# Writing a window mask on the score products' own 64x32 tiles instead of on 64x128 tiles

## The chip, the cores and the metric

One core of a Trainium2 chip (trn2). The metric is the device time of one execution in microseconds (us). TensorE has its own row in the profile for matmuls (PE) and one for weight loads (PEld), which overlap.

## The reference

The input is x of 8 sequences, 256 tokens, 128 channels. First comes one pre-norm causal attention with 16 heads of 8 channels and position slopes. Then the main part, six layers deep, each with local attention and a feed-forward:

```python
# attn_layer, per layer, 16 heads of 64
q, k, v = split(shift_tokens(x) @ Wqkv, 3)
q, k = l2norm(q) * q_scale, l2norm(k) * k_scale        # then rotary tables
# local_attention, windows of 32 queries, each sees its own 32 keys and the 32 before
mask = (it < jb) | (it > jb + w) | (jb == -1)
sim = einsum('bhwie,bhwje->bhwij', bq, bk2) * 8.0
sim = where(mask, -finfo.max, sim)
out = einsum('bhwij,bhwje->bhwie', softmax(sim), bv2)
x = out @ Wo + x
# ffn_layer: layernorm, W1, gelu gate, W2, + x
```

What matters here is `sim` with its mask: a query of a window may see at most 64 keys, of which the mask takes about half away, and in the first window of a sequence also the missing keys before it.

## The kernel before, in words

All loops are written out by Python, so the program is one long straight line of instructions for each engine; there is no loop on the chip. The setup part (lines 212 to 1178) computes the first attention and folds weights. The main part handles 48 units, one for each layer and sequence (`UNITS = L * B`), in a software pipeline: `pipeline` calls `step` for s from -1 to 50, and each engine's `step` names, by hand and in a fixed order, which piece of which unit comes next. Four units are under way at a time: `after` (s + 1), `u` (s), `before` (s - 1) and `last` (s - 2).

A unit has 256 tokens in two tiles of 128 tokens, called the first tile (t = 0) and the second tile (t = 1) here. For each tile TensorE does:

- `proj` (lines 1767 to 1790): a 128x512 piece of the q, k or value projection, as three products (lines 1784, 1785, 1786) that accumulate in one PSUM bank;
- `transpose_qk` (line 1801): four 128x128 transposes of the rotated q or k, which ScalarE copies to `qT` and `kT` (`copy_qkT`, lines 1590 and 1594);
- `scores` (lines 1804 to 1823): the masked scores of the tile in two PSUM banks, `SO[t]` and `SO[t] + 1`, one for the even and one for the odd heads (`hp`);
- `transpose_p` (line 1831) and `values` (line 1842): transposes of the probabilities and their products with the values, on 128x32 tiles;
- the feed-forward of an older unit (lines 1853 to 1903).

In `scores` a pair of heads lies on the 128 partitions, head `hp` on partitions 64 hp to 64 hp + 63. A window of 32 queries fills 32 columns of the array, so a score product takes 64 rows and 32 columns of it: eight such 64x32 tiles exist, two row halves by four column tiles `k`, and 8 pairs of heads `a` times 4 windows `k` times 2 halves `hp` make 64 products of 64 columns each. They don't start from zero. Before them, the mask is written to the whole of both banks by two products, one for each row half, with a one-hot matrix `wpick` (bf16) that picks for each of the 128 queries its row of the mask table `wmask` (bf16, 8 x 64 = 512 columns). These open the accumulation (`start=True`), and the scores add to it (`start=False`).

The waits at the head of `scores` (lines 1809 and 1811) are for the last copy to `kT` of this tile by ScalarE (`qkT_a`) and for the copy of the attention output out of the same banks for the unit before (`o_a`). At its end one signal (`sc_p`) releases `soft_top` on VectorE (line 1422), the row maximum of the scores; then follow subtraction (line 1431), exponential on ScalarE (line 1602), sum (line 1439) and scaling on VectorE. In TensorE's hand-written order `scores(u, 0)` stands at line 1948 between `proj(u, 1, 6)` and `proj(u, 1, 7)`, and `scores(u, 1)` at line 1969 between `proj(after, 0, 4)` and `proj(after, 1, 4)`.

Of the kernel before, what the change touches and what calls it, by code (L numbers as in the profile page):

```python
# [83 lines left out]
def build(nc, x, w_heads, bq_heads, bk_heads, w_v, b_v_rows, w_proj, b_proj_rows, wqk, q_scale_rows, k_scale_rows, wvt, wo,  # L84
          feed_cols, w1, w2, rope, ident, win_mask, win_pick, causal, positions, slope_heads, one_row, weights, out):
    with ExitStack() as ctx:
        def sb(name, shape, dt=F32):
            return ctx.enter_context(nc.sbuf_tensor(name, shape, dt))
# [4 lines left out]
        ps = ctx.enter_context(nc.psum_tensor("ps", [P, 8, 512], F32))  # L93
# [10 lines left out]
        wmask = sb("wmask", [P, PAIRS, 2 * WIN], BF16)  # L104
        wpick = sb("wpick", [P, TT, P], BF16)
# [36 lines left out]
        PJ, SO, TP, FB = 0, (2, 4), 6, 7  # L142
# [1049 lines left out]
        def index(u):  # L1192

            return u[0] * 2 + u[1]
# [5 lines left out]
        def live(u):  # L1200

            n = index(u)
            return not isinstance(n, int) or 0 <= n < UNITS
# [7 lines left out]
        with nc.Block() as block:  # L1211
# [531 lines left out]
            def _(pe):  # L1743
                M = nc.tensor
# [59 lines left out]
                def scores(u, t):  # L1804

                    if not live(u):
                        return
                    n, par = index(u), u[1] % 2
                    pe.wait_ge(qkT_a.sem, qkT_a.at(n, 4 * t + 3))
                    if not (isinstance(n, int) and n < 1):  # L1810
                        pe.wait_ge(o_a.sem, o_a.at(n - 1, t))
                    for hp in range(2):
                        rows = slice(64 * hp, 64 * hp + 64)
                        M.matmul(ps[:, SO[t] + hp, :], wpick[rows, t, :], wmask[rows, :, :].rearrange("p a k -> p (a k)"), start=True, stop=False)  # L1814
                    for a in range(PAIRS):
                        for k in range(4):
                            w = 4 * t + k
                            for hp in range(2):
                                rows = slice(64 * hp, 64 * hp + 64)
                                out_s = ps[32 * k:32 * k + 32, SO[t] + hp, a * 2 * WIN:(a + 1) * 2 * WIN]  # L1820
                                last = M.matmul(out_s, qT[rows, par, a, 32 * w:32 * w + 32], kT[rows, a, 32 * w:32 * w + 64],  # L1821
                                                start=False, stop=a == PAIRS - 1)
                    last.then_inc(sc_p.sem, 1)
# [259 lines left out]
```

## Time and profile before

| | |
|---|---|
| three runs | 1713.82, 1719.82, 1723.14 us; median 1719.82 |
| span of the profiled execution, its own time on the profiler | 1711.8 us |
| TensorE matmuls (PE) | busy 1660.6 us, 97% of the span, 26531 records |
| weight loads (PEld) | busy 1330.2 us, 78% |
| VectorE (DVE) | busy 1480.6 us, 86% |
| ScalarE (ACT) | busy 1268.7 us, 74% |
| GpSimd (POOL) | busy 1283.8 us, 75% |
| mean granted clock of TensorE | 0.991 |

The profile comes from one execution; its span runs from the first to the last instruction, and the time of a run has what lies around the span on top. For the profiled execution no other time than the span is given. Durations of single matmuls overlap on the array, so on PE the distance from one start to the next tells what a product costs. A float32 product shows as two records (64 score products as 128), a bf16 product or a float32 transpose as one.

### The profile page before, as it was taken

What the parts mean: (1) busy time and instruction counts of PE and PEld (TensorE: products, weight loads), DVE (VectorE), ACT (ScalarE), POOL (GpSimd) and SP (SyncE); (2) the same over time, 40 slices, a digit from 0 to 9 for tenths busy, and PEclk for the clock granted to TensorE, in tenths of its full rate; (3) what the DMA queues carried; (4) which work ended last, traced back from release to release, by engine and by line L of the source; (5) the groups of instructions that cost most, each with busy time, mean ns of one, the idle gap of its engine ahead of it and who ended that gap; (6) DMA issues with size and microseconds to landing.
All of it is one profiled execution on the core that took longest, in us unless ns stands there. A gap on an engine that the chain in (4) does not pass through costs nothing.

```text
span 1711.8 us, 65044 instructions
## 1 busy us (share of the span) xinstructions
PE 1660.6 (97%) x26531; PEld 1330.2 (78%) x26531; DVE 1480.6 (86%) x2313; ACT 1268.7 (74%) x2639; POOL 1283.8 (75%) x1744
## 2 busy tenths in 40 slices
PE   7999959999999999999999999999999999999997
PEld 5777637878888888888788888888878887888885
DVE  6887748989999999999889999999989898999984
ACT  6888746767777777777777777777777777777774
POOL 7787568777777877777778777787877777777770
PEclk9999979999999999999999999999999999999999
DMA  3588516564866656765567756658565567656654
GB/s 123 189 289 315 183 37 150 123 149 105 241 136 147 147 116 152 207 158 135 125 141 196 168 138 137 143 121 236 123 161 127 132 142 205 155 132 138 143 119 118
DMA packets 101385, 265.43 MB, mean 155 GB/s; under 512 B 26720, under 2 KB 34912, under 8 KB 101088
## 3 DMA queue, kind: packets, MB, share of 16 engines
q1 hardware_dynamic: 101088, 261.26, 60.6%
q8 instruction: 211, 3.46, 0.9%
q14 instruction: 86, 0.70, 0.1%
HBM read 45.15 MB, written 27.26 MB: 42 GB/s over the span
## 4 chain that ended last, share of the span: by engine, by line
PE 80%; issue 2%; SPq 1%; DVE 1%; ACT 1%; POOL 1%; DMA 1%; ACTq 0%; DVEq 0%; POOLq 0%
PE ps L1784 12%; PE ps L1801 10%; PE ps L1786 10%; PE ps L1842 10%; PE ps L1785 10%; PE ps L1821 8%; PE ps L1892 7%; PE ps L1831 5%; PE ps L1903 4%; PE ps L1814 2%; SPq L1228 1%; PE ps L1861 1%; PE ps L1869 1%; PE ps L1853 1%; PE ps L1878 1%
## 5 line engine op out<-in xcount | busy, mean ns | idle before, releaser
L1312 POOL TENSOR_TENSOR rot<-rot 128x512 f32<-128x512 f32 x380 | 480.7, 1287 | 99.6 <-DVE rot L1411 99.6
L1411 DVE TENSOR_TENSOR rot<-ps,rope_l 128x1024 f32<-128x1024 f32 x380 | 463.3, 1221 | 48.2 <-ACT sq L1568 33.4
L1578 ACT ACTIVATE un<-ps 128x512 f32<-128x512 f32 x384 | 229.5, 598 | 238.1 <-PE ps L1786 205.3
L1784 PE MATMUL ps<-w_t,xs_hi 128*128 128x512 f32 x764 | 377.4, 494 | 19.2 <-PEq L362 11.0
L1355 POOL TENSOR_TENSOR rot<-rot,rnorm 128x1024 f32<-128x1024 f32 x190 | 362.1, 1906 | 21.4 <-POOL rnorm L1339 0.4
L1786 PE MATMUL ps<-w_t,xs_lo 128*128 128x512 f32 x764 | 303.4, 397 | 0.4 <-issue 0.4
L1785 PE MATMUL ps<-w_t,xs_hi 128*128 128x512 f32 x764 | 301.5, 395 | 1.6 <-issue 1.6
L1568 ACT ACTIVATE sq<-ps 128x512 f32<-128x512 f32 x380 | 227.0, 601 | 60.3 <-PE ps L1786 59.9
L1397 DVE TENSOR_REDUCE ssum<-sq 128x16 f32<-128x1024 f32 x190 | 230.8, 1215 | 27.4 <-ACT sq L1568 27.4
L1801 PE MATMUL ps<-ident_s,rot 128*128 128x128 f32 x1536 | 236.9, 277 | 3.3 <-ACT kT L1594 1.7
L1801 PEld LDWEIGHTS ps<-ident_s,rot 128*128 128x128 f32 x1536 | 178.5, 140 | 52.1 <-issue 22.6
L1784 PEld LDWEIGHTS ps<-w_t,xs_hi 128*128 128x128 f32 x764 | 144.4, 189 | 64.0 <-DVE rot L1411 18.3
L1842 PE MATMUL ps<-vk,pT 128*32 128x128 f32 x6144 | 187.6, 274 | 0.8 <-ACT pT L1611 0.8
L1842 PEld LDWEIGHTS ps<-vk,pT 128*32 128x32 f32 x6144 | 161.8, 110 | 17.2 <-issue 15.7
L1786 PEld LDWEIGHTS ps<-w_t,xs_lo 128*128 128x128 f32 x764 | 144.1, 189 | 34.9 <-issue 1.2
L1785 PEld LDWEIGHTS ps<-w_t,xs_hi 128*128 128x128 f32 x764 | 145.9, 191 | 11.7 <-issue 2.4
L1821 PEld LDWEIGHTS ps<-kT,qT 64*32 64x32 f32 x12288 | 133.8, 106 | 27.1 <-issue 26.3
L1821 PE MATMUL ps<-kT,qT 64*32 64x64 f32 x12288 | 151.1, 227 | 3.2 <-issue 3.2
L1422 DVE TENSOR_REDUCE smax<-ps 128x16 f32<-128x1024 f32 x96 | 117.6, 1225 | 42.2 <-PE ps L1821 42.2
L1892 PE MATMUL ps<-xg,w_s 128*128 128x256 f32 (+1 forms) x576 | 149.6, 383 | 0.7 <-DVE hid L1487 0.3
L1439 DVE TENSOR_REDUCE lsum<-ps 128x16 f32<-128x1024 f32 x96 | 116.6, 1215 | 3.2 <-ACT ps L1602 3.2
L1431 DVE TENSOR_TENSOR prob<-ps,smax 128x1024 f32<-128x1024 f32 x96 | 117.1, 1220 | 1.5
(139 smaller groups left out, 3013.9 us busy)
## 6 DMA issues: line engine op xcount, KB each, us to landing
vk<-un SPq DMA_DIRECT2D x1440, 128.0 KB
w_t<-weights_dram SPq DMA_DIRECT2D x48, 512.0 KB, 6.5
weights_dram<-rot SPq DMA_DIRECT2D x12, 1024.0 KB, 5.2
weights_dram<-sq SPq DMA_DIRECT2D x24, 512.0 KB, 4.3
raw<-wqk_dram SPq DMA_DIRECT2D x24, 256.0 KB, 4.5
wvt_s<-wvt_dram SPq DMA_DIRECT2D x12, 256.0 KB, 5.3
wo_s<-wo_dram SPq DMA_DIRECT2D x12, 256.0 KB, 5.8
w_s<-w_dram SPq DMA_DIRECT2D x6, 341.0 KB
```

The costliest lines, as they stand in the source:

```text
L1312: last = G.tensor_tensor(cos[:, :, s, :], cos[:, :, s, :], sin[:, :, 1 - s, :], ALU.add)
L1355: G.tensor_tensor(v, v, rnorm[:, t, kind * H:(kind + 1) * H, None].broadcast_to([P, H, D]), ALU.mult).then_inc(nrm_g.sem, 1)
L1397: V.tensor_reduce(ssum[:, t, kind * H:(kind + 1) * H], sq[:, kind, :].rearrange("p (h e) -> p h e", h=H), AX_X, ALU.add).then_inc(ss_d.sem, 1)
L1411: V.tensor_tensor(dst, src[:, None, :, :].broadcast_to([P, 2, H // 2, D]), tab[:, :, None, :].broadcast_to([P, 2, H // 2, D]), ALU.mult).t ...
L1578: S.activation(un[:, (u[1] % 2) * TT + t, j // 2, (j % 2) * HALF:(j % 2 + 1) * HALF], ps[:, PJ + PJ_BANK[t][QK_BANKS + j], :], ACT.Copy).t ...
L1784: M.matmul(bank, x_hi, w_t[:, j, 0, :], start=True, stop=False)
L1785: M.matmul(bank, x_hi, w_t[:, j, 1, :], start=False, stop=False)
L1786: last = M.matmul(bank, x_lo, w_t[:, j, 0, :], start=False, stop=True)
L1801: last = M.transpose(ps[:, TP, a * P:(a + 1) * P], rot[:, kind, 0, c * P:(c + 1) * P], ident_s[:, :])
L1821: last = M.matmul(out_s, qT[rows, par, a, 32 * w:32 * w + 32], kT[rows, a, 32 * w:32 * w + 64], start=False, stop=a == PAIRS - 1)
L1842: last = M.matmul(ps[32 * k:32 * k + 32, SO[t], 0:C], pT[:, a, 32 * k:32 * k + 32], vk[:, 4 * t + k, a, :], start=a == 0, stop=a == PAIRS - 1)
L1892: last = M.matmul(ps[0:rows, feed_bank(n, i), g * T:(g + 1) * T], w1_s[:, g * DI + at:g * DI + at + rows], xg[:, :], start=True, stop=True)
```

## The change

The two mask products of a tile become eight. Each writes the mask for one window (`k`) and one row half (`hp`), on the 64x32 tile of the array on which the score products of that window and half follow, to 32 partitions of the same bank. The moving operand is the same, all 512 columns of it, in each. The values written are the same, the order of everything else too; all waits and signals stay.

```diff
@@ scores(u, t)
                     pe.wait_ge(qkT_a.sem, qkT_a.at(n, 4 * t + 3))
                     if not (isinstance(n, int) and n < 1):
                         pe.wait_ge(o_a.sem, o_a.at(n - 1, t))
-                    for hp in range(2):
-                        rows = slice(64 * hp, 64 * hp + 64)
-                        M.matmul(ps[:, SO[t] + hp, :], wpick[rows, t, :], wmask[rows, :, :].rearrange("p a k -> p (a k)"), start=True, stop=False)
+                    for k in range(4):
+                        for hp in range(2):
+                            rows = slice(64 * hp, 64 * hp + 64)
+                            M.matmul(ps[32 * k:32 * k + 32, SO[t] + hp, :], wpick[rows, t, 32 * k:32 * k + 32],
+                                     wmask[rows, :, :].rearrange("p a k -> p (a k)"), start=True, stop=False)
                     for a in range(PAIRS):
                         for k in range(4):
                             w = 4 * t + k
```

## Rows read from the trace of the kernel before

**Rows 1.** The page, part 1: busy us (share of the span) and instructions.

```profile
PE 1660.6 (97%) x26531; PEld 1330.2 (78%) x26531; DVE 1480.6 (86%) x2313; ACT 1268.7 (74%) x2639; POOL 1283.8 (75%) x1744
```

**Rows 2.** The page, part 4: the chain that ended last, by engine and line.

```profile
PE 80%; issue 2%; SPq 1%; DVE 1%; ACT 1%; POOL 1%; DMA 1%; ACTq 0%; DVEq 0%; POOLq 0%
```

**Rows 3.** A steady stretch: length, then busy us of PE, PEld, DVE, ACT, POOL.

```profile
500.00:600.00 100.00, 99.99 (x1650) 82.38 (x1652) 91.97 (x109) 76.92 (x138) 79.21 (x103) 1.00 0.62 143
```

**Rows 4.** PE by line and shape: total busy us, mean ns | idle before.

```profile
L1821 PE MATMUL ps<-kT,qT 64*32 64x64 f32 x12288 | 151.1, 227 | 3.2 <-issue 3.2
L1814 PE MATMUL ps<-wmask,wpick 64*128 64x512 bf16 x192 | 37.8, 391 | 0.0
```

**Rows 5.** Timeline, PE, a first-tile block: start, us to last end, engine, line, operation.

```profile
811.33 0.39 PE L1785 MATMUL ps<-w_t,xs_hi 128*128 128x512 f32 x1
811.56 0.40 PE L1786 MATMUL ps<-w_t,xs_lo 128*128 128x512 f32 x1
811.89 0.39 PE L1814 MATMUL ps<-wmask,wpick 64*128 64x512 bf16 x2
812.21 1.48 PE L1821 MATMUL ps<-kT,qT 64*32 64x64 f32 x128
813.62 0.50 PE L1784 MATMUL ps<-w_t,xs_hi 128*128 128x512 f32 x1
```

**Rows 6.** The same block, line 1821 alone, in short windows (records touching each window).

```profile
812.19:812.27 0.08, 0.06 (x8) 0.07 (x14) 1.00 0.00 0
812.27:812.33 0.06, 0.06 (x15) 0.06 (x23) 1.00 0.00 0
```

**Rows 7.** Timeline, PE: transposes (1831, 1801) and values (1842).

```profile
807.33 0.60 PE L1801 MATMUL ps<-ident_s,rot 128*128 128x128 f32 x4
807.86 1.95 PE L1842 MATMUL ps<-vk,pT 128*32 128x128 f32 x64
...
818.01 1.03 PE L1831 MATMUL ps<-ident_s,prob 128*128 128x128 f32 x8
818.89 0.38 PE L1801 MATMUL ps<-ident_s,rot 128*128 128x128 f32 x2
```

**Rows 8.** Timeline, ACT: the copy of kT ahead of four blocks.

```profile
270.83 0.60 ACT L1594 ACTIVATE kT<-ps 128x512 f32<-128x512 f32 x1
...
616.05 0.59 ACT L1594 ACTIVATE kT<-ps 128x512 f32<-128x512 f32 x1
...
810.43 0.60 ACT L1594 ACTIVATE kT<-ps 128x512 f32<-128x512 f32 x1
...
1669.76 0.59 ACT L1594 ACTIVATE kT<-ps 128x512 f32<-128x512 f32 x1
```

**Rows 9.** Timeline, PE: three blocks, each with what follows its scores.

```profile
272.38 1.48 PE L1821 MATMUL ps<-kT,qT 64*32 64x64 f32 x128
273.79 0.51 PE L1784 MATMUL ps<-w_t,xs_hi 128*128 128x512 f32 x1
...
617.34 1.63 PE L1821 MATMUL ps<-kT,qT 64*32 64x64 f32 x128
618.89 0.51 PE L1784 MATMUL ps<-w_t,xs_hi 128*128 128x512 f32 x1
...
1670.41 0.39 PE L1814 MATMUL ps<-wmask,wpick 64*128 64x512 bf16 x2
1670.73 1.70 PE L1821 MATMUL ps<-kT,qT 64*32 64x64 f32 x128
1672.36 0.33 PE L1853 MATMUL ps<-ident_s,o 128*128 128x128 f32 x1
```

**Rows 10.** Timeline, PE: a stall in a first-tile block; the page, part 3: instruction fetches.

```profile
873.92 1.36 PE L1821 MATMUL ps<-kT,qT 64*32 64x64 f32 x114
876.07 0.34 PE L1821 MATMUL ps<-kT,qT 64*32 64x64 f32 x14 [0.78 <-issue]
...
q8 instruction: 211, 3.46, 0.9%
```

## The prediction

> **What bounds the kernel now.** I read first the busy shares, then the chain of work that ended last, then the steady stretches, and last the timeline of TensorE around one scores block. TensorE is busy for 97% of the span, with DVE at 86% next [rows 1]; PE holds 80% of the chain [rows 2]; in a steady stretch of 100 us it is busy for 99.99 us at the full granted clock (1.00, which is 2.4 GHz), and DVE for 92 [rows 3]. So TensorE sets the end, and what a block costs there is its start to start distance on PE, not its durations, which overlap: the two mask products read 391 ns each, 37.8 us in all, and the score products 227 ns each, 151.1 us in all with 128 records per block, two for each of its 64 products [rows 4]. A step has two blocks: the first tile (t = 0) and the second (t = 1), 96 in the kernel, 48 of each.
>
> One block of the first tile reads as follows [rows 5]. The last projection product starts at 811.56, where its neighbours stand 0.23 us apart (811.33 to 811.56). The mask pair starts at 811.89, so 0.33 later: 0.10 more than a neighbour's distance. The scores start at 812.21, 0.32 after the pair, though both mask products started together and 512 columns take 0.23. That is 0.09 more. After the 128 score records the next projection starts at 813.62. The same excess stands where transposes on the full array are followed by values on 128x32 tiles: eight transposes take 0.88 to the next block of the same shape (818.01 to 818.89), so 0.11 each, but four take 0.53 to the first value product (807.33 to 807.86), which is 0.09 over 4 x 0.11 [rows 7]. I read it as the price of a change of tile shape, some 0.09 each (estimate). So today a block pays for three changes: full array to 64x128, 64x128 to 64x32, 64x32 to full array.
>
> **The change, part by part.** (1) The change of shape between mask and scores goes. Before: 0.32 us from first mask product to first score product. After: the stream alone, 0.23 by the projection rows [rows 5], since each score tile then waits only for the mask on its own 64x32 tile. The nearest row for what could be added is the first weight load on a small tile, which nothing covers: 8 score records lie in the first 0.08 us, and 7 of the next round are in by 0.06 later (x15 counts those still running too) [rows 6], so 0.02. If the masks pay it in the scores' place the scores' first round loses it, and nothing is added in sum; if both pay it, the gain is 0.07; if the bf16 stream is a little shorter than the projection's and the scores' load is covered as well, 0.10. I take 0.09, the middle, with ends 0.07 and 0.10. The two other changes of shape stay, at the price that they have.
>
> (2) Six more products and six more weight loads per block, 12 instructions, 1152 in all. On the array they cost nothing if the eight run side by side, four column tiles in each of two row halves. For it: score records on just these eight tiles start 8 in 0.08 us, with durations above 0.2 [rows 4, 6]; 64 value records of 128 columns on four column tiles take 1.95 us, 30 ns each, where full-array transposes of 128 columns need 0.11 each [rows 7]; and the mask pair on two row halves starts together. Not shown anywhere: eight streams of 512 bf16 columns at once. Bounds: nothing, and eight in line only by row half, 4 x 0.23 = 0.92 instead of 0.23. I take nothing, by the score rows, which are the same tiles.
>
> (3) The issue of those 12 instructions. The masks wait for the copy of kT by ScalarE; what follows in TensorE's queue is issued only after it. In the first tile that copy ends at 810.43 + 0.60 = 811.03, so 1.18 us before the scores start; in the second at 616.05 + 0.59 = 616.64, 0.70 before they start at 617.34 [rows 8, 9]. The block itself, from first score to next product, takes 1.41 in the first tile (813.62 - 812.21) in nearly all steps, but 1.55 in the second (618.89 - 617.34) [rows 5, 9]; going through its 48 blocks in the same view I find a few at 1.41 and most at some 0.12 over it. At the very end the lead is 0.38 (1670.35 to 1670.73) and the block 1.63; at the start one with a lead of 0.95 (271.43 to 272.38) reads 1.41 again. So with a short lead the issue falls behind the array: 0.22 late at a lead of 0.38, 0.12 at 0.70, nothing from 0.95 on. The rate: 4 + 256 instructions lie between 1670.35 and the next product at 1672.36 [rows 9]; without 0.1 for the change of shape at the end that is about 7 ns each (estimate), so 12 cost 0.085.
> First tile: lead 1.18 - 0.09 - 0.085 = 1.0, still above 0.95: no loss, gain 0.09 x 48 = 4.3 us.
> Second tile: lead 0.70 - 0.09 - 0.085 = 0.52. Between the two points (0.10 more for 0.32 less) that makes 0.06 more lateness, so the gain is 0.09 - 0.06 = 0.03, x 48 = 1.5 us. Ends: 0.09 if the lateness has another cause, and a loss of 0.085 if every instruction counts in full.
>
> (4) Nothing is added to any wait, semaphore or DMA of the data, and the waits in front of the masks stay where they are. Scores that end 0.09 earlier only feed DVE earlier, which has slack of 8 in 100 us [rows 3]; if DVE became late next, it would cost the part of 0.09 that it can't take, not more. The instructions are fetched by DMA, 16 KB at a time (3.46 MB in 211), and in some blocks PE stands for it, as 0.78 us before 876.07 [rows 10]. Going through the timeline I count some nine such stalls, about 8 us together, nearly all in or right behind a scores block. The change shifts where these pieces begin and adds 4 or 5 of them. I put it at nothing with 3 us to either side.
>
> **Sum.** 4.3 + 1.5 = 5.8 us, 0.34%. The profiled execution spans 1711.8; the three runs read 1713.82 to 1723.14, so the shortest lies 2.0 above the span and the median 8.0. I take the change from the median: 1719.8 - 5.8 = 1714.0 us. About 0.5% (8.6 us) is what a measurement of this kernel can tell from no change.
>
> **The rivals.**
> A, the forecast: full gain in the first tile, a third of it in the second. 1714.0; its own range with the ends above and the fetch's 3 us is 1708 to 1720. Chance 0.44.
> B: the second tile's lateness is not one of issue, or the queue has caught up before the scores start; both tiles gain 0.09 to 0.10, 96 x 0.095 = 9.1 us, 1710.7. For it: a few second-tile blocks already read 1.41 with the same lead. Against it: the blocks with short leads are the late ones. Chance 0.26.
> C: the issue decides the second tile in full: 48 x (0.09 - 0.085) = 0.2 us, 1719.6, no change. For it: with issue as the bound the mask's stream time is worth nothing there. Against it: the last block issues in less time than most. Chance 0.15.
> D, slower: the eight mask streams don't run side by side, so that the four column tiles of a row half follow each other. It decides in the distance from first mask to first score: above 0.32 us the change loses. At 0.92 it is 0.60 x 96 = 57.6 us more, 1777. Half way, with two at a time, 0.46 gives 13 us more, 1733. For it: the masks bring 512 columns for each weight load of 32, four copies of one stream from the same partitions, where a score product brings 64. Against it: the tiles' records of scores and values [rows 6, 7]. Chance 0.07.
> E: the shifted pieces of the code meet the dense blocks more often, twice the stalls of today, 8 - 5.8 = 2 us more, 1722, or 1727 with a stall for each of the 5 added pieces as well. For it: the blocks get denser by 12 instructions in 260. Against it: the stalls sit where the pieces happen to begin, and a shift moves as many out as in. Chance 0.05.
> F, slower too: the issue of one product with its weight load takes up to 0.06 us, which is what lies, change of shape included, between the end of the kT copy (1670.35) and the first mask product (1670.41) in the last block [rows 8, 9]. Then six more are 0.36: the second tile loses 0.36 - 0.09 = 0.27, 13 us over 48 blocks, and the first tile's lead falls to 1.18 - 0.09 - 0.36 = 0.73, where 0.1 of lateness eats its gain. 1733. Against it: 64 products are through in 1.41 us, 22 ns each with their weight loads [rows 5]. Chance 0.03.
> This is the case that the Trainium skill, "TensorE: Matmul & The Clock Gate" (in "Wait — 56ns, not 53.3ns?"), would make the likely one: it says that without hardware decoding the sequencer spends about 62 ns on each matmul, and that this binds once the array's work is shorter. By that figure the six would be 0.37 us a block. The trace doesn't agree, with its 22 ns for a product.
>
> **How the numbers follow.** The likeliest single case is A: 1714.0. Range 1706 to 1725: it takes in A, B, C and most of E with the runs' own spread of some 4 us about a median, and leaves out D, F and the tails, under 2 in 10. Faster by over 8.6 us: B's upper half and what the fetch adds to A, 0.27. Slower by over 8.6 us: D, F and the tail of E, 0.12. Within: 0.61.
>
> **What would show it.** In the timeline after, eight mask records start within 0.06 us, 0.33 behind the last projection product, and the first score 0.23 to 0.25 behind the first mask (0.32 now): step 1 and 2. If it is 0.4 or more, D. The block of the first tile stays 1.41 and that of the second grows from some 1.53 to 1.59: step 3; if it doesn't grow, B; if it grows by 0.17, C. Idle time put down to issue stays near today's. PE stays busy for 99 of 100 us in steady stretches. The prediction is wrong if PE waits for DVE more often, or if the changes of shape that stay become dearer than 0.10.

## The result, and the profile after

The changed kernel takes 1726.8 us (median of 11 runs, 1724.76 to 1735.04) against 1718.1 us for the kernel before in runs beside it: ratio 1.0061, 95% interval 1.0045 to 1.0077. The forecast was 1714.0 with a range of 1706 to 1725. So it is slower by 0.6%, where a gain of 0.3% was forecast, and it lies outside the range. A trace is of one execution: the two profiled ones differ by 12.2 us (1711.8 and 1724.0), the medians by 8.7.

The page of the changed kernel: its parts 1, 4 and 3, then a steady stretch (columns as in [rows 3]) and the two forms of the scores by line and shape (columns as in [rows 4]). The mask is now line 1815, the scores are line 1823, the values line 1844.

```profile
PE 1655.3 (96%) x27107; PEld 1340.0 (78%) x27107; DVE 1480.7 (86%) x2313; ACT 1267.7 (74%) x2639; POOL 1281.4 (74%) x1744
PE 82%; issue 2%; DVE 1%; ACT 1%; POOL 0%; ACTq 0%; DVEq 0%; POOLq 0%
q8 instruction: 216, 3.54, 0.9%
```

```profile
500.00:600.00 100.00, 99.96 (x1762) 83.17 (x1746) 92.46 (x111) 76.07 (x137) 79.89 (x107) 1.00 0.65 149
```

```profile
L1823 PE MATMUL ps<-kT,qT 64*32 64x64 f32 x12288 | 151.6, 225 | 14.9 <-issue 14.9
L1815 PE MATMUL ps<-wmask,wpick 64*32 64x512 bf16 x768 | 39.5, 389 | 0.0
```

Against [rows 1] PE has 576 more records and is busy for 5 us less in a span that is 12 us longer. The steady stretch is as full as in [rows 3]. The one row that differs plainly from [rows 4] is the idle time in front of score products: 14.9 us put down to "issue", where it was 3.2. The views of waits, PE alone, 240 to 1660 us, say how often (us in total, times, longest); first the kernel before, then the changed one:

```profile
PE ps L1821 <- issue: 3.2, 6, 0.8
```

```profile
PE ps L1823 <- issue: 14.9, 13, 2.3
```

Blocks without such a wait did what was meant. The timeline of PE in the changed kernel, a first-tile and a second-tile block:

```profile
880.35 0.40 PE L1786 MATMUL ps<-w_t,xs_lo 128*128 128x512 f32 x1
880.68 0.41 PE L1815 MATMUL ps<-wmask,wpick 64*32 64x512 bf16 x8
880.90 1.46 PE L1823 MATMUL ps<-kT,qT 64*32 64x64 f32 x128
882.29 0.50 PE L1784 MATMUL ps<-w_t,xs_hi 128*128 128x512 f32 x1
...
833.49 0.40 PE L1786 MATMUL ps<-w_t,xs_lo 128*128 128x512 f32 x1
833.82 0.41 PE L1815 MATMUL ps<-wmask,wpick 64*32 64x512 bf16 x8
834.04 1.76 PE L1823 MATMUL ps<-kT,qT 64*32 64x64 f32 x128
835.74 0.50 PE L1784 MATMUL ps<-w_t,xs_hi 128*128 128x512 f32 x1
```

The eight masks are one group of 0.41 us, the length of a single one: they run side by side. Mask to score is 0.22 where [rows 5] have 0.32. From the last projection product to the next one, the median of the 48 first-tile blocks falls from 2.060 to 1.942 us, that of the second-tile blocks from 2.177 to 2.117. That is 48 x (0.118 + 0.060) = 8.5 us gained in the ordinary case.

**Where the time went.** A block that waits looks like this: timeline of PE, then PE's rows in windows (columns as in [rows 3]), of the changed kernel.

```profile
1440.24 0.41 PE L1815 MATMUL ps<-wmask,wpick 64*32 64x512 bf16 x8
1440.46 1.50 PE L1823 MATMUL ps<-kT,qT 64*32 64x64 f32 x120
1443.69 0.32 PE L1823 MATMUL ps<-kT,qT 64*32 64x64 f32 x8 [1.73 <-issue]
1443.94 0.50 PE L1784 MATMUL ps<-w_t,xs_hi 128*128 128x512 f32 x1
...
1444.92 0.63 PE L1784 MATMUL ps<-w_t,xs_hi 128*128 128x512 f32 x1
1445.35 0.63 PE L1785 MATMUL ps<-w_t,xs_hi 128*128 128x512 f32 x1
1445.78 0.63 PE L1786 MATMUL ps<-w_t,xs_lo 128*128 128x512 f32 x1
```

```profile
1440.00:1441.70 1.70, 1.70 (x128) 1.41 (x128) 1.65 (x4) 0.60 (x1) 1.29 (x6) 1.00 0.93 210
1441.70:1443.70 2.00, 0.27 (x27) 0.11 (x11) 0.17 (x1) 0.00 (x0) 1.86 (x2) 1.00 0.48 104
1443.70:1447.20 3.50, 3.50 (x18) 2.75 (x19) 1.55 (x2) 1.20 (x2) 3.42 (x4) 0.62 0.89 201
```

The view of DMA for 1441.02 to 1442.31, then for 1442.31 to 1443.68 (packets, MB, share of 16 engines):

```profile
q8 instruction: 1, 0.02, 6.0%
...
q1 hardware_dynamic: 32, 0.11, 36.0%
```

Queue q8 brings TensorE's instructions in pieces of 16 KB. I numbered PE's instructions (a weight load and a product each, and the waits and signals) and found that every long wait at a block stands at one and the same place of a 256-instruction period: that is the length of a piece. I call it a boundary. The count fits the queue's: 54192 instructions make 211 boundaries before and 55344 make 216 after, and q8 has 211 and 216 packets ([rows 10] and the page above). In this block one boundary is crossed at 1439.92 and the next at 1441.75. The fetch for the piece behind the second begins at 1441.04, which is 1.12 after the first crossing, and ends at 1442.29; PE goes on at 1443.69, 1.40 later.

A piece of 256 instructions usually lasts some 7 us. A block has 272 of them in 1.9 us (260 before the change). So where two boundaries fall into or close around one block, the next piece isn't there yet. Counting waits over 0.6 us in or right behind a block (from one product's start to the next), the kernel before has 9 (8.9 us in all), the changed one 16 (26.0 us).

There is a second price, which the last group of rows above shows: behind this wait the projection products stand 0.43 apart, not 0.23, and the granted clock is 0.62 for 3.5 us (the level of 1.2 GHz for most of it). Adding up every 10 us window from 260 to 1660 us whose granted clock is below 0.97, the changed kernel lacks 6.8 us of full clock, the kernel before nothing. All of it lies behind waits of 1.9 us and more; waits of about 1 us left the clock at 1.00. Not every long wait costs it: two at 457 and 699 us left it up, and so did one of 2.2 us for weights in the kernel before.

From the third to the 93rd block the two traces differ by 13.0 us (1356.1 and 1369.1). Waits over 0.62 us, less 0.4 each for the distance that would be there anyway, make 14.6 of it (7.8 and 22.4); the rest of the blocks gives 6.4 back; what is left, 4.8, lies in the projections and their neighbours, at the lower clock.

### The profile page after: what moved, and what is told of

Same layout as the page of the kernel before. It is cut to its first block, busy times and chain, and to the rows that moved or that the text cites. A ratio compares the mean times of both kernels' runs of the same rounds, so it can differ in the third digit from the quotient of the medians.

```text
span 1724.0 us, 66196 instructions
## 1 busy us (share of the span) xinstructions
PE 1655.3 (96%) x27107; PEld 1340.0 (78%) x27107; DVE 1480.7 (86%) x2313; ACT 1267.7 (74%) x2639; POOL 1281.4 (74%) x1744
## 4 chain that ended last, share of the span: by engine, by line
PE 82%; issue 2%; DVE 1%; ACT 1%; POOL 0%; ACTq 0%; DVEq 0%; POOLq 0%
PE ps L1784 12%; PE ps L1801 11%; PE ps L1844 10%; PE ps L1786 10%; PE ps L1785 10%; PE ps L1823 8%; PE ps L1894 7%; PE ps L1833 5%; PE ps L1905 4%; PE ps L1815 2%; PE ps L1863 1%; PE ps L1871 1%; PE ps L1855 1%; PE ps L1880 1%; DVE rot L1411 0%
## 5 line engine op out<-in xcount | busy, mean ns | idle before, releaser
L1823 PE MATMUL ps<-kT,qT 64*32 64x64 f32 x12288 | 151.6, 225 | 14.9 <-issue 14.9
L1823 PEld LDWEIGHTS ps<-kT,qT 64*32 64x32 f32 x12288 | 147.0, 105 | 22.2 <-issue 16.0
L1785 PEld LDWEIGHTS ps<-w_t,xs_hi 128*128 128x128 f32 x764 | 146.9, 192 | 13.6 <-issue 3.9
```

What stands on the lines that cost most here:

```text
L1785: M.matmul(bank, x_hi, w_t[:, j, 1, :], start=False, stop=False)
```

## The experiments

Names that begin with a_ are made from the changed kernel, b_ from the kernel before. Below "waits" are those over 0.6 us in or right behind a block, 96 blocks each, from the profiled execution; the ratio is to the kernel before on the same chip. The rows come from several chips, so medians of different rows are set side by side only where the text says that the chip is the same. A count can be one more or less, by how far "right behind" reaches.

| kernel | median us | ratio, 95% interval | waits | their sum, us |
|---|---|---|---|---|
| before | 1718.1 | | 9 | 8.9 |
| changed | 1726.8 | 1.0061, 1.0045 to 1.0077 | 16 | 26.0 |
| a_jump | 1730.76 | 1.007, 1.0052 to 1.0089 | 18 | 22.6 |
| b_jump | 1718.44 | 1.0, 0.9983 to 1.0016 | 5 | 6.1 |
| b_pad12 | 1788.33 | 1.0402, 1.0377 to 1.0428 | 18 | 32.3 |
| a_shift | 1737.25 | 1.0102, 1.0083 to 1.0122 | 20 | 26.2 |
| b_len | 1841.03 | 1.073, 1.0705 to 1.0754 | 16 | 24.3 |
| b_shift2 | 1729.05 | 1.0076, 1.0048 to 1.0103 | 9 | 10.9 |
| a_jump2 | 1744.35 | 1.0171, 1.0146 to 1.0196 | 10 | 13.3 |
| b_jump2 | 1724.28 | 1.0053, 1.0034 to 1.0073 | 3 | 3.8 |
| a_jump3 | 1717.93 | 0.9999, 0.9986 to 1.0013 | 10 | 16.3 |
| b_jump3 | 1716.67 | 0.9988, 0.9976 to 1.0 | 6 | 7.9 |
| a_later | 1736.96 | 1.0112, 1.0093 to 1.013 | 20 | 29.2 |
| a_later_jump | 1724.48 | 1.0035, 1.0021 to 1.0049 | 8 | 13.7 |
| b_later | 1726.44 | 1.0062, 1.004 to 1.0084 | 11 | 10.6 |
| a_copy | 1720.71 | one run | 18 | 23.5 |
| a_jump4 | 1716.05 | 0.998, 0.9964 to 0.9996 | 3 | 6.5 |
| b_jump4 | 1713.32 | 0.9975, 0.9961 to 0.9988 | 3 | 2.1 |
| a_jump5 | 1718.46 | 0.9999, 0.9985 to 1.0014 | 7 | 11.6 |
| b_jump5 | 1720.31 | 1.0012, 0.9994 to 1.0029 | 7 | 12.3 |

**Moving the boundaries with idle signals: a_jump, b_jump.** Idle signals in the projections and just ahead of the masks, at eleven (four) places, so that the boundaries jump over the part of a block where they hurt.

```diff
+                PADS = {(2, 0): 22, (7, 0): 56, ...}
+                def pay(times):
...
+                        pe.sem_inc(padding.sem, 1)
```

> The kernel after, with 508 instructions that do nothing but count up an unused semaphore, put in small groups between the scores blocks of 12 of the 96, so that no boundary of a 16 KB piece of TensorE's instructions (256 instructions) falls from 30 instructions before a block's first mask to 34 behind it, nor in its last 50. Theory F (the time lost is waiting for the next piece, when the dense block runs from one boundary to the next before that piece is fetched): the stalls of over 0.6 us in and behind the blocks, 16 in the trace of after with about 22 us together, are gone; 1727 - 20 = about 1706 us. Rival L (longer program: each added piece costs, wherever it begins): two more pieces, 1728 or more. Rival Q (the block itself is dearer, by issue or by the array): unchanged, 1727.

> The kernel before with the same means: 282 idle instructions in four places keep the boundaries away from the blocks. Theory F: its 9 stalls, about 8 us, go, 1718 - 8 = 1710, so that a_jump is 4 to 8 us faster than this one: that difference is what the change does without the fetch (0.12 us less in a first-tile block, 0.06 in a second-tile one, by the medians of the two traces: 8.5 us). Rival L: 1719. Rival Q: a_jump is slower than this one.

The table's counts mislead here. A row of idle signals right behind a block is itself a distance of over 0.6 us: nine of a_jump's 18 waits are such rows (7.1 us) and four of b_jump's 5. At a boundary in a block a_jump has 8 waits (12.2 us) and one more mixed with signals (3.4 us), where the changed kernel has 16, and b_jump has 1 where the kernel before has 9. Six of the 8 stand where the boundary comes some 223 instructions into the block, just at the edge of the last 50 that were to stay free. So the waits did fall by place, but the 508 signals cost more than they saved, as the next pair shows, and the times decide nothing between the theories.

**The same instructions without the masks' work, and a shift alone: b_pad12, a_shift.** b_pad12 puts twelve idle signals in front of the two masks of the kernel before, the number that the change adds. a_shift puts 128 of them at the program's start, so that all boundaries of the changed kernel move by half a period.

```diff
+                    for _ in range(12):
+                        pe.sem_inc(padding.sem, 1)
```

> The kernel before, two mask products, with 12 idle instructions in front of each block's waits: as many instructions for a step as in the kernel after, and the same wandering of the boundaries, but the dense part of a block stays 260 instructions long instead of 272. Theory F with the dense part's length as cause: some 9 to 12 stalls as in before, 1718 to 1722. Rival P (position: the boundaries happened to fall better before): 16 stalls and over 20 us in them as in after, 1735. Rival L: like P, at least 5 us more than before.

> The kernel after, with 127 idle instructions at its very start, where TensorE waits for the first input, so that every boundary lies half a piece elsewhere. Theory F: as the boundaries wander by 40 instructions a step through all positions, 18 instead of 25 blocks have one within their window, so 12 to 16 stalls, other blocks, 1720 to 1727. Rival P: it changes by 10 us or more to either side. Rivals L and Q: unchanged, 1727.

PE by line and shape, b_pad12:

```profile
L1824 PE MATMUL ps<-kT,qT 64*32 64x64 f32 x12288 | 153.2, 226 | 18.9 <-issue 18.8
L1817 PE MATMUL ps<-wmask,wpick 64*128 64x512 bf16 x192 | 37.9, 382 | 36.9 <-issue 33.8
```

The signals themselves cost 0.68 us in each first-tile block (from the last projection product to the first mask 1.004 us in the median, 0.329 before), so 56 ns each beyond what hides beside the product before them, and 33.8 us of idle time ahead of the masks in all, which spoils the time as a measure. The waits still say something: with two masks, but a step as long as the changed kernel's, there are 18, as many as with eight. a_shift's start has a wait of its own:

```profile
PE ps L994 <- issue: 22.7, 1, 22.7
```

Its first mask starts 14.6 us later than in the changed kernel, which has nothing to do with the blocks. Its main part, first mask to last, is 1436.8 us against 1439.8 in the changed kernel and 1428.0 before, with 20 waits of 26.2 us. So a shift by half a period brings back 3.0 of the 11.8 us at most, and no wait: where its pieces begin was not what made the changed kernel slow.

**Length of a step, or the place of the boundaries: b_len, b_shift2.** b_len adds idle weight loads to eight projections of each step of the kernel before, which makes its steps 1064 instructions long, as the changed kernel's; b_shift2 adds 128 of them once.

```diff
+                    def idle():
+                        if (t, j) in ((1, 0), (1, 1), ...):
+                            M.ldweights(wpick[:, 0, :])
...
+                PADS = {(2, 0): 64, (2, 1): 64}
```

> The kernel before, two mask products, with 24 idle weight loads a step (128x128 bf16, one ahead of each product of eight projections far from the blocks): as many instructions for a step as in the kernel after, the same wandering of the boundaries, the dense part 260 instructions. The idle semaphore counts of the first runs cost TensorE some 55 ns each and so hid what they were for; a weight load should hide beside the product before it. Theory F with the density as cause: stalls as in before, 9 or so with 9 us, 1719 us plus what the weight loads cost. Rival P2 (the step's length, 1064 instructions instead of 1040, sets how many stalls there are): 16 or more stalls with over 20 us, 1733 or more.

> The kernel before with 128 idle weight loads in one unit near the start, so that all later boundaries lie half a piece elsewhere. Theory F by density: again about 9 stalls, 1718 to 1722. Rival P (9 stalls were luck of position): 14 or more, 1728.

b_len has 16 waits of 24.3 us with blocks of 260 instructions, b_shift2 9 of 10.9 us. An idle weight load, 97 ns in the profile, doesn't hide behind a projection product: b_len is 126 us above before for 1140 of them and 15 us of waits, which leaves 97 ns each, and b_shift2's 128 make 12 of its 13.6 us by that. Both times are those of the filler. In both kernels, as in the kernel before, 6 blocks have a boundary from 9 instructions ahead of the first mask to 6 behind it; 6 and 5 of them wait, 4 in the kernel before. b_len's other ten waits have the boundary 12 to 38 instructions ahead of the first mask or deep in the block.

**Jumps with idle weight loads: a_jump2, b_jump2.**

```diff
+                PADS = {(2, 0): 34, (7, 0): 56, (11, 1): 75, ...}
...
+                    for _ in range(times):
+                        M.ldweights(wpick[:, 0, :])
```

> The kernel after with 649 idle weight loads in ten places far from the blocks, so that no boundary falls from 46 instructions before a block's first mask to 29 behind it, from unit 2 on. Theory F: stalls in the blocks go from 16 to 3 or fewer, 26 us to under 4; 1727 - 22 plus the weight loads' own cost, at most 649 x 0.05 = 30 us and nearer 5: 1710. If the loads turn out dear, the stalls' count and sum in the trace decide. Rivals L and Q: 1727 and more.

> The kernel before with 210 idle weight loads in four places, to the same end. Theory F: its stalls in blocks, 9 us, go; 1719 - 8 + some 2 = 1713, and a_jump2 beats it by some 3 to 8 us, as the change saves 0.12 and 0.06 us a block once the fetch is out of the way. Rival Q: a_jump2 is slower than this.

The waits fall to 10 and 3, by place as meant; 649 and 210 weight loads are dearer than what they save.

**Jumps with idle products of one column: a_jump3, b_jump3, and the scores one projection later: a_later, a_later_jump.** The idle products lie on the values' 128x32 tiles and write one column that the first value product overwrites.

```diff
+                IDLE = {(1, 0): 4, (1, 1): 4, (7, 0): 7, ...}
...
+                    for i in range(IDLE.get((n + 1, t), 0)):
+                        k = i % 4
+                        M.matmul(ps[32 * k:32 * k + 32, SO[t], 0:1], pT[:, 0, 32 * k:32 * k + 32], vk[:, 4 * t + k, 0, 0:1],
+                                 start=True, stop=True)
```

```diff
                     proj(after, 0, 4)
-                    scores(u, 1)
                     proj(after, 1, 4)
+                    scores(u, 1)
```

> The kernel after, with 71 idle one-column products (284 instructions) on the values' own 128x32 tiles, ahead of the values in ten places, so that no piece of TensorE's instructions begins from 18 instructions before a block's first mask to 28 behind it. In after and a_shift nearly every block with a boundary from 9 before to 18 behind stalled, 13 and 15 of them; none of 96 would here. Theory F: 3 to 6 stalls in blocks are left (those from a late fetch), 26 us fall to some 6; the idle products cost about 10 x 0.3 = 3 us; 1727 - 17 = 1710. Rivals L and Q: 1727 to 1730.

> The kernel before with 23 such products in five places, no boundary from 16 before to 10 behind. Theory F: its stalls inside this window (6, about 6 us) go: 1718 - 5 = 1713, and a_jump3 is 2 to 6 us faster than this kernel, since the change without the fetch saves 8.5 us by the blocks' medians. Rival Q: a_jump3 slower than this by 5 us or more.

> The kernel after with scores(u, 1) one projection later, behind proj(after, 1, 4): the copy of kT then ends about 1.07 us before the masks of the second tile start instead of 0.38. Theory I (the second tile's block is longer because its instructions are issued late): its block falls from a median of 1.42 to 1.25 us, as in the first tile, 48 x 0.17 = 8 us less, 1719, if the stalls stay at some 26 us. Rival (transfers that run beside the second tile's block slow it): it stays at 1.42, and the kernel at 1727.

> Both: scores(u, 1) one projection later, and 70 idle products that keep the boundaries away. Theories F and I together: 1727 - 17 - 8 = 1702, faster than before and after. If one of them falls, its part is missing: 1710 without I, 1719 without F.

These fillers cost next to nothing: 71 products in a_jump3, and the changed kernel comes down to the time of before (0.9999). But 10 waits stay, nine of them in blocks that were brought to begin some 16 instructions behind a boundary, so that the next one comes some 240 instructions into them. (The expectation for a_jump3 gives 15 waiting blocks for a_shift from 9 before to 18 behind; its trace has 10, and all 10 wait.)

a_later was to test step 3 of the prediction. The copy of kT now ends some 1.07 us ahead of the second tile's masks, 1.3 ahead of its scores, more than the 0.95 from which the prediction expected no lateness. The block didn't get shorter: from first to last score record start its median is 1.487 us (1.420 in the changed kernel, 1.244 in the first tile). So the lead over the copy is not what makes the second tile's block long. With 20 waits the kernel is slower; a_later_jump takes 12 of them away and 12.5 us with them.

**Wider margins: a_jump4, b_jump4.** As a_jump3 and b_jump3, with more idle products (162 and 52), so that blocks land some 45 instructions behind a boundary. They stand ahead of the value products; the text on record says "projections", which is wrong.

> The changed kernel; 162 idle one-column products stand before eleven projections, so placed that every dense block of scores (8 + 32 products, 272 instructions) begins at least 30 instructions behind, or at least 45 ahead of, the instruction at which TensorE goes from one 16 KB piece of its instructions to the next; in a_jump3 the blocks landed 16 to 18 ahead of it and nearly all that landed there stalled. Theory P (the loss is TensorE waiting for the next piece, where two pieces end within the 1.5 us of a dense block): at most 3 stalls over 600 ns at blocks after the first round, waits over 650 ns in the main part under 28 us against 43 in the changed kernel, and the time 1706 to 1714 us, below both kernels, as the medians of the blocks are 8.6 us better than before. Rival L (the stalls follow the length of the program, not the place of the boundaries): 14 to 20 stalls remain and the time is 1724 to 1730. Rival S (the fetch is slow for other traffic, wherever the boundary lies): 8 to 12 stalls, 1716 to 1722.

> The kernel before with the same care for its dense blocks (2 + 32 products, 260 instructions): 52 idle one-column products before four projections. Theory P: the six blocks that lay in the window don't any more, stalls at blocks fall from 9 to 3 or fewer, and the time is 1710 to 1715 us, some 5 us under the kernel before. a_jump4 should be 2 to 8 us faster than this one, which is what the eight products are worth with the stalls out of both. Rival L: 9 stalls remain, 1716 to 1721, and a_jump4 is not faster.

Both are faster than the kernel before, and so than the changed one: b_jump4 by 0.25%, a_jump4 by 0.2%, and both intervals lie below 1. The waits are 3 and 3, so neither the program's length nor a constant share of slow fetches explains the others: place it is. But a_jump4 reads 2.7 us more than b_jump4 on the same chip, where 2 to 8 less was expected; the intervals of the two ratios overlap, so which of them is faster isn't shown. The timeline of a_jump4 shows two things, here the idle products and the block after them, and another block:

```profile
413.90 0.48 PE L1846 MATMUL ps<-vk,pT 128*32 128x1 f32 x35
...
416.74 0.63 PE L1850 MATMUL ps<-vk,pT 128*32 128x128 f32 x11 [0.80 <-issue]
...
419.67 1.15 PE L1825 MATMUL ps<-kT,qT 64*32 64x64 f32 x97
421.44 0.46 PE L1825 MATMUL ps<-kT,qT 64*32 64x64 f32 x31 [0.62 <-issue]
...
690.59 1.15 PE L1825 MATMUL ps<-kT,qT 64*32 64x64 f32 x97
694.84 0.68 PE L1825 MATMUL ps<-kT,qT 64*32 64x64 f32 x31 [3.09 <-issue]
```

The idle products are so dense themselves (36 records start within 0.31 us) that a boundary waits there. And the second block waits 3.1 us (from 691.53 on) though the boundary before it was crossed at 686.57, 5.0 us earlier. Its windows (columns as in [rows 3]) and the view of DMA from 687.7 to 691.9:

```profile
687.70:692.20 4.50, 4.05 (x126) 3.13 (x127) 2.92 (x4) 3.33 (x6) 2.60 (x9) 1.00 0.97 364
692.20:693.30 1.10, 0.00 (x0) 0.00 (x0) 0.00 (x0) 0.00 (x0) 1.10 (x1) 1.00 1.01 398
694.80:697.00 2.20, 2.16 (x35) 1.70 (x35) 1.39 (x2) 0.00 (x0) 2.12 (x2) 0.50 0.03 11
```

```profile
q1 hardware_dynamic: 415, 1.51, 96.4%
```

The data's DMA fills all 16 engines at 364 GB/s, no instruction piece is among its packets, and the fetch begins only at 692.43, 5.86 us after that boundary. It ends at 693.48 and PE goes on at 694.84, 1.36 later, at a clock of 0.50. From the third block to the 93rd the blocks of a_jump4 take 6.2 us less than b_jump4's (159.4 and 165.6 us with their waits, 154.1 and 165.0 without). Elsewhere a_jump4 takes more: 3.5 us in the value products (some 2 on the idle products, the rest on waits), 2.7 in the transposes of q and k, 1.7 around the feed-forward and the transposes of the output, so that the whole stretch is 1.4 us longer. At the clock, counted as above, it lacks 3.4 us and b_jump4 none. So the changed block keeps its gain where no wait falls, but no run here turns that gain into a time below b_jump4's.

**The control for a_later, and the copies of v: b_later, a_copy.** b_later moves the second tile's scores in the kernel before as a_later does. a_copy leaves most of the copy of v out, 64 columns of each row remain; it has one run, and nothing is concluded from its time.

```diff
-                                src = un[32 * k:32 * k + 32, (n % 2) * TT + tile, hp, :]
-                                sp.dma_start(vk[lo:lo + 32, w, :, :].rearrange("p a c -> p (a c)"),
-                                             src).then_inc(vk_in[t].sem, 16)
+                                src = un[32 * k:32 * k + 32, (n % 2) * TT + tile, hp, 0:64]
+                                sp.dma_start(vk[lo:lo + 32, w, 0, 0:64], src).then_inc(vk_in[t].sem, 16)
```

> The kernel before with scores(u, 1) put one projection later, as in a_later: the control for it. Theory P: the boundary's place against the 260-instruction blocks takes values that the kernel before didn't show, and stalls stand from about -9 to +6 instructions and not above +10, where a_later's 272-instruction blocks stalled to +18; the time goes with their count, 0.9 to 1.2 us for each. Theory T (the second tile's block is longer because of what runs beside it, not because its kT is late): its block's median stays near 1.5 us although kT is 1 us early; if lateness of kT were the cause it would fall to 1.25 to 1.3 us.

> The changed kernel with each copy of v into the values' array cut to 64 columns a row: it leaves out most of the copy of v, so its values are wrong. One look at what makes the second tile's block of scores longer than the first's (1420 against 1244 ns). Theory T (the copies' traffic beside it): the second tile's median falls to within 60 ns of the first's, 1240 to 1300. Rival: it stays at 1380 to 1430, and the cause is in TensorE's own order of work or in the drains of the tiles. The count of stalls at boundaries should stay at 12 to 18 if they hang on the boundaries' place alone, and fall below 10 if a fetch is slow because of these copies.

b_later: the second tile's median is 1.373 us (1.384 before), so again the lead over kT doesn't matter. Seven of its eleven waits stand where a boundary comes from 11 instructions ahead of a block's first mask to 5 behind it, near what I expected; the other four, with the boundary some 200 to 240 instructions into the block, were not expected. a_copy: the second tile's median stays at 1.420, that of the changed kernel, so the traffic of these copies isn't what lengthens it, and 18 waits stay. Theory T fell. The second tile's block loses its time towards its end: in the last third of its score records the starts stand 14.0 ns apart in the changed kernel and 12.7 before, where the first tile's have 10.3 in both, and in the changed kernel the middle third has 11.1 in place of 9.4. Why is open.

**Idle products away from the blocks: a_jump5, b_jump5.** The idle products (72 and 29) move to the transposes of the probabilities, and the blocks nearest to a boundary begin some 20 instructions behind it.

```diff
                     pe.wait_ge(pn_d.sem, pn_d.at(n, t))
+                    for i in range(IDLE.get((n + 1, t), 0)):
+                        k = i % 4
+                        M.matmul(ps[32 * k:32 * k + 32, SO[t], 0:1], ident_s[:, 32 * k:32 * k + 32], ident_s[:, 0:1],
+                                 start=True, stop=True)
```

> The changed kernel with 72 idle one-column products ahead of ten groups of prob's transposes, some 200 instructions before the block of scores that they move, so that no block begins less than 28 instructions behind a boundary of the pieces or less than 19 ahead of one. a_jump4's four stalls at blocks all stood where a block began 48 instructions behind a boundary whose other side held the idle products (36 passes in 0.31 us) and the values' products. Theory P' (what counts is the time between two boundaries against the fetch, and the idle products themselves made a dense stretch there): placed apart from the block they cost no such stall; 0 to 3 stalls at blocks after the first round, and the time 1709 to 1714 us, below before, changed kernel and b_jump4. Rival Q (a landing 16 to 20 ahead of a boundary stalls by its place, as in a_jump3): 6 to 10 stalls and 1717 to 1722. Rival F (late fetches behind full DMA engines come wherever the boundary lies): 3 to 5 stalls and 1714 to 1717.

> The kernel before with the same placing, 29 idle products ahead of four groups of prob's transposes, no block less than 13 behind or 19 ahead of a boundary. Theory P': 0 to 3 stalls at blocks, 1711 to 1714 us, as b_jump4 or 1 us less; a_jump5 comes out 1 to 6 us under it, what is left of the 8.6 us. Rival W (the time saved at the blocks is waited for elsewhere): the two come out within 2 us of each other, though the blocks of a_jump5 sum to 8 us less.

7 waits in each, and no gain over before: rival Q by the count. All seven in a_jump5 and three in b_jump5 stand at such a landing, at the next boundary some 236 instructions into the block; three blocks of a_jump5 that land there don't wait. From the boundary ahead of the block to PE's last product before the wait 3.1 to 3.35 us pass in all of a_jump5's seven, so an ordinary fetch is just late. With about the same waits in both (11.6 and 12.3 us), a_jump5 reads 1.9 us less than b_jump5; the intervals of their ratios overlap, so that is no measurement of the eight products' worth.

**The rule behind all of them.** I took the 201 waits at blocks in these 20 traces for which a fetch begins behind the boundary before. From the end of that fetch to PE's next product it is 1.40 us in the median, and 1.22 to 1.61 in nine of ten. The fetch takes 0.9 to 1.9 us, 1.1 in the median. Over all boundaries of the main part of a trace it begins 0.9 to 1.1 us after the boundary before in the median, but one in ten begins more than 2.7 to 4.5 us after it. Where the DMA engines were at least 85% busy in the first 1.5 us after a boundary, 26% of the fetches began over 2 us late (2015 boundaries); where they were under 30% busy, 12% (1349). So an ordinary piece needs about 1.0 + 1.1 + 1.4 = 3.5 us from the boundary before, and a late one up to 8. The instructions of a block pass in 1.9.

**What the twelve instructions do, by place.** The same traces answer what share the longer block has. I give a boundary's place in instructions from a block's first mask, and leave out the three kernels with idle signals at the blocks (a_jump, b_jump, b_pad12). From +7 to +18, where a second boundary falls inside a block of 272 instructions or within 2 of its end, but behind one of 260, 21 of 21 blocks of the changed form wait (nine kernels, 39.3 us), and 1 of 27 of the form before (eight kernels, 0.8 us). b_len, whose step is as long as the changed kernel's, has 4 such blocks and none waits. From -9 to +6 both forms wait: 27 of 33 and 21 of 25. In the changed kernel itself 6 blocks stand from +7 to +18 and wait 12.5 us; in the kernel before 4 do and wait 0.8. That is 11.7 of the 17.1 us that the waits grew by. Of the three kernels left out, b_pad12 doesn't fit (below, under what is not settled).

The Trainium skill, "Runtime: NRT & Kernel Launch" (in "Instruction fetch mechanics"), says that instructions are refilled in blocks of 16 KiB, 256 instructions, by a DMA queue that the sequencer drives, and that crossing a boundary is mostly hidden, since dispatch is slower than the fill. The traces agree with the size and the queue. They don't agree with the hiding: by that rule the waits would cost nothing, and they cost 26.0 us in the changed kernel. The same section of the Trainium skill says too that PE holds 2048 instructions, and in a note beside it that the memory is only two blocks; what is seen here, a fetch that starts behind the boundary before and is waited for at the next, is how the smaller number would behave. No run here shows how many it holds.

## Why the prediction was wrong

**What bounds the kernel** was right: PE is still 82% of the chain and no other engine became late.

**Step 1**, the change of shape between mask and scores: right. Forecast 0.09 (0.07 to 0.10), measured 0.319 to 0.227, so 0.092. The blocks of the first tile gained 0.118, more than the step: the scores' own stretch is shorter as well (1.266 to 1.244).

**Step 2**, eight streams at once at no cost: right. The eight start within 23 ns, and rival D has nothing for it.

**Step 3**, the issue of twelve instructions, second tile: the size was near (0.06 gained where 0.03 was forecast; from first score to next product the block grew from 1.53 to 1.57 us, forecast 1.59), the mechanism was wrong. "With a short lead the issue falls behind the array" rested on four blocks; a_later and b_later lengthened the lead and the block stayed long. Rival F is out too: an added product with its weight load costs no 0.06 us where the eight masks start within 23 ns.

Steps 1 to 3 came to 5.8 us, measured 8.5. Rival C's 1719.6 was summed wrongly, apart from all this: its 0.2 us is the second tile's alone, and with the first tile's 4.3 it would have been 1715.3.

**Step 4 failed.** It read: "The change shifts where these pieces begin and adds 4 or 5 of them. I put it at nothing with 3 us to either side." Measured: 17.1 us more of waits at blocks (26.0 - 8.9), and up to 6.8 us lost to the lower clock behind the longest of them. The rows for it were at hand: [rows 10] show such a wait, and the prediction had counted nine, "nearly all in or right behind a scores block". What was missing is the question why there. A piece is 256 instructions; the block before had 260, which is just over one piece, the new one 272. Two boundaries can fall inside one block when the first comes within its first 4 instructions (260 - 256) before, within its first 16 after. With the same margin ahead of it, the part of the period in which nearly every block waits grew by those 12, from about -9 to +6 to about -9 to +18: 13 blocks have a boundary in it and 12 of them wait, where it was 6 and 4. By the width of the part, 28 of 256 places for 96 blocks, 10 or 11 blocks would be there on average; a_shift has 10. So some of the 13 is chance of place, most of it isn't. The sentence against rival E, "a shift moves as many out as in", holds for a shift and not for a longer block: shifted by half a period, a_shift has as many waits.

Rival E had the right mechanism and almost the right price (twice the stalls, 1722 or 1727; measured 1726.8 with 16 for 9), at a chance of 0.05. Its price still was too low for each wait: 1.6 us on average against 1.0 before, since the blocks with two boundaries inside wait longest (12.5 us in the six from +7 to +18), and the clock behind them wasn't in it. That the sum of E came out near is partly luck, as the gain of the blocks was taken too low.

**What is not settled.** 11.7 of the 17.1 us go with the block's 12 instructions; where the other 5.4 come from isn't shown. b_len and b_pad12 have 16 and 18 waits with blocks of 260 instructions, in kernels whose fillers changed more than the length of the step. Most of what they have too many stands where a boundary is 10 to 38 instructions ahead of the first mask; there 41 of 68 blocks of the changed form wait and 21 of 53 of the form before (from -30 to -10), so a wait at that place isn't certain in either. In b_pad12 3 of the 4 blocks with a boundary from +7 to +18 wait too, with two masks; the twelve signals ahead of them are the one difference, and why they should matter there is open. Late fetches explain single ones, as at 691.5 us in a_jump4. And the waits were counted in one execution of each kernel.

## What to carry to other kernels

Where a straight-line program has a stretch that issues 256 PE instructions in less than about 3.5 us, count the instructions of that stretch against 256 before counting cycles: each instruction added there widens the part of the period in which PE waits 1 to 4 us for its own code, and a wait near 2 us can cost the clock for 3 more. A change that saves array time by more and smaller products has to be priced with that. A few idle one-column products can move a boundary away from such a stretch for some 9 ns a record, as long as they don't make a dense stretch of their own.

## What the runs showed that I had not expected

- The clock: after a wait of 2.0 us (1441.75 to 1443.69) the granted clock was 0.62 over 3.5 us and products stood 0.43 apart; in a_jump4 it read 0.50 after 3.3 us of standing.
- A piece that is in is not yet usable: 1.40 us pass from the end of its transfer to the next product.
- Fillers are not alike: an idle signal ahead of the masks cost PE 56 ns, an idle bf16 weight load of 128x128 in the projections 97 ns, an idle one-column float32 product about 17 ns (two records of 9).
- Idle signals in a row start 151 ns apart. a_shift's, ahead of the setup part, run from 3.2 to 22.1 us with nothing beside them and delay the start by 14.6 us; in b_pad12 all but 56 ns of each hid beside the product before.
